# Attention softmax on one core: every second group's block maxima joined on GpSimd, head by head, instead of on VectorE

## What is computed

```python
q = (x @ Wq + bq).reshape(1, B * N, H, hd)             # 2048 queries, H = 16 heads, hd = 16
kv = (cond @ Wkv + bkv).reshape(1, -1, 2, H, hd)       # 2048 keys and values
...
attn = jnp.einsum('bhqk,bhkd->bhqd', q, k)             # each query against all 2048 keys
attn = jax.nn.softmax(attn.astype(jnp.float32), axis=-1)
attn = _fq_unsigned(attn, axis=-1)                     # rounded to 0..255 of the row's largest weight
out = jnp.einsum('bhqk,bhkd->bhqd', attn, v)
```

## Time and profile before

| | |
|---|---|
| median of 3 runs | 1166.4 us (1164.74 to 1167.02) |
| the profiled execution: its own time | 1166.14 us |
| its span, first to last instruction | 1164.4 us |
| busy over the span | PE 90%, DVE 82%, ACT 77%, POOL 60% |
| busy from 300 to 400 us | PE 86.77, DVE 98.11, ACT 98.44, POOL 80.50 us of 100 |
| granted TensorE clock from 300 to 400 us | 1.00 of full |
| first and last exponential of the attention | 85.6 and 722.3 us |

### The profile page before, as it was taken

How to read it: one execution, slowest core, us unless ns; L and a number is a source line. 1 busy time by engine, 2 the same in 40 slices (tenths; PEclk the granted TensorE clock), 3 DMA queues, 4 the chain that set the end, 5 groups by cost and what they waited for, 6 DMA issues and landing times.

```text
span 1164.4 us, 24047 instructions
## 1 busy us (share of the span) xinstructions
PE 1048.7 (90%) x8281; PEld 606.3 (52%) x8396; DVE 950.6 (82%) x1748; ACT 891.8 (77%) x1546; POOL 701.3 (60%) x625
## 2 busy tenths in 40 slices
PE   8988888888888888888888889899998999999997
PEld 4743444444444444444444447656654465557775
DVE  6999999999999999999999996863336788953335
ACT  4779999999999999999999996734543576834441
POOL 3016888888777878888788776447651000753332
PEclk9999999999999999999999999899999999999999
DMA  6697998888888889888876764856938001523336
GB/s 193 120 163 149 173 172 162 169 169 171 167 172 175 165 166 170 178 162 170 155 118 111 115 109 78 243 170 181 321 115 331 0 1 46 178 84 109 97 97 233
DMA packets 388799, 176.36 MB, mean 151 GB/s; under 512 B 330413, under 2 KB 373650, under 8 KB 388680
## 3 DMA queue, kind: packets, MB, share of 16 engines
q1 hardware_dynamic: 381976, 157.85, 62.1%
q0 software_dynamic: 6480, 16.77, 4.3%
q10 hardware_dynamic: 224, 0.20, 0.1%
HBM read 52.70 MB, written 43.59 MB: 83 GB/s over the span
## 4 chain that ended last, share of the span: by engine, by line
PE 49%; DVE 28%; ACT 13%; issue 5%; DMA 2%; POOL 2%; SPq 1%; ACTq 0%; POOLq 0%; DVEq 0%
DVE top L426 22%; ACT weight L485 10%; PE bank L220 8%; PE bank L234 8%; PE bank L1187 4%; PE bank L2616 4%; PE bank L1580 3%; PE bank L252 3%; PE bank L2632 3%; PE bank L1166 2%; PE bank L1174 2%; PE bank L1853 1%; PE bank L1598 1%; PE bank L682 1%; POOL dispatched_rows L1823 1%
## 5 line engine op out<-in xcount | busy, mean ns | idle before, releaser
L485 ACT ACTIVATE weight<-bank,bias,sq_all 128x1024 uint8<-128x1024 f32 x512 | 609.9, 1201 | 24.0 <-PE bank L234 18.7
L426 DVE TENSOR_REDUCE top<-bank 128x1 f32<-128x512 f32 (+1 forms) x683 | 610.2, 951 | 11.5 <-PE bank L220 1.1
L537 POOL CAST weight<-turned 128x2048 bf16<-128x2048 uint8 x256 | 478.8, 1892 | 41.0 <-PE bank L252 22.2
L234 PE MATMUL bank<-kT,query 128*128 128x512 bf16 x917 | 284.1, 382 | 26.4 <-ACT weight L485 12.2
L252 PEld LDWEIGHTS bank<-v_sb,weight 128*128 128x128 bf16 x4096 | 172.0, 96 | 102.7 <-POOL weight L537 0.5
L220 PE MATMUL bank<-kT,qspace 64*128 64x512 bf16 x687 | 135.0, 387 | 55.8 <-DVE top L426 55.8
L252 PE MATMUL bank<-v_sb,weight 128*128 128x16 bf16 x4096 | 172.6, 170 | 0.8 <-POOL weight L537 0.4
L220 PE MATMUL bank<-kT,query 128*128 128x512 bf16 x329 | 124.8, 379 | 2.1 <-DVE top L426 1.4
L234 PEld LDWEIGHTS bank<-kT,query 128*128 128x128 bf16 x1024 | 59.9, 97 | 103.9 <-ACT weight L485 61.9
L1823 POOL DMA_INDIRECT dispatched_rows<-qspace,put x32 | 37.1, 1160 | 116.0 <-DVE qspace L2373 106.9
L485 ACT ACTIVATION_READ_ACCUMULATOR weight<-bank,bias,sq_all 128x1 f32 x512 | 101.7, 199 | 0.0
(11 more groups left out here) (352 smaller groups left out, 1471.7 us busy)
## 6 DMA issues: line engine op xcount, KB each, us to landing
dispatched_rows<-zeros SPq DMA_DIRECT2D x32, 524.0 KB, 3.1
answered_rows<-zeros SPq DMA_DIRECT2D x16, 512.0 KB, 3.2
late<-answered_rows SPq DMA_DIRECT2D x16, 512.0 KB, 6.3
erow<-dispatched_rows SPq DMA_DIRECT2D x39, 131.0 KB, 2.1
wgu<-in_L_ffn_w_gate SPq DMA_DIRECT2D x26, 176.0 KB, 3.8
wgu<-in_L_ffn_w_up SPq DMA_DIRECT2D x26, 176.0 KB, 3.7
query<-qspace SPq DMA_DIRECT2D x32, 128.0 KB, 3.1
turned<-weight SPq DMA_TRANSPOSE x256, 3.1
```

The costliest lines, as they stand in the source:

```text
L234: mm = pe.matmul(unit[u % 2][:, v * 512:(v + 1) * 512], query2[:, t % 2, h, :], kT[:, h // 2, first + v * 512:first + (v + 1) * 512], star ...
L426: ve.tensor_reduce(top[:, first:first + count], bank[:, first % 3:first % 3 + count, :], AX.X, ALU.max).then_inc(s_max, 1)
L485: ac.activation(weight8[:, n % BYTES, u * 1024:(u + 1) * 1024], unit[u], ACT.Exp, bias=bias[:, n:n + 1], scale=sq_all[:, n:n + 1], accum_o ...
L537: po.tensor_copy(weight[:, n % 3, :, :, :].rearrange("p c q two -> p (c q two)"), turned8[:, n % 3, :, :].rearrange("p c q -> p (c q)").bi ...
```

## The change

The groups with an even number are joined as before. Of a group with an odd number (32 of 65), VectorE's line 430 is gone, and so is GpSimd's multiplication of line 520. In their place GpSimd waits for VectorE's last reduction of that group, and then handles each head by itself, on one column per operation: the maximum of three block columns (one as the tensor, two as scalars per partition), and, after a wait for the last of these, the maximum with the fourth column times the negative scale (again two scalars per partition). The addition of ln 255 stays one operation for the group.

```diff
-            group_end = {last_reduction(NBLOCK * (n0 + k) - 1): (n0, k) for n0, k in group_of}
+            group_end = {last_reduction(NBLOCK * (n0 + k) - 1): (n0, k) for n0, k in group_of[::2]}
...
                 n0, k = group_of[i]
                 sh = shift[:, n0:n0 + k]
-                po.wait_ge(s_shift, i + 1)
-                po.tensor_tensor(sh, sh, nsq_all[:, n0:n0 + k], ALU.mult).then_inc(s_scaled, 1)
+                if i % 2 == 0:
+                    po.wait_ge(s_shift, i // 2 + 1)
+                    po.tensor_tensor(sh, sh, nsq_all[:, n0:n0 + k], ALU.mult).then_inc(s_scaled, 1)
+                else:
+                    po.wait_ge(s_max, last_reduction(NBLOCK * (n0 + k) - 1) + 1)
+                    columns = {n: [top[:, 2 * NBLOCK * (n // 2) + 2 * b + n % 2:][:, 0:1] for b in range(NBLOCK)] for n in range(n0, n0 + k)}
+                    for n in range(n0, n0 + k):
+                        m = po.tensor_scalar(shift[:, n:n + 1], columns[n][0], columns[n][1], columns[n][2], ALU.max, ALU.max)
+                    m.then_inc(s_joined, 1)
+                    po.wait_ge(s_joined, i // 2 + 1)
+                    for n in range(n0, n0 + k):
+                        m = po.tensor_scalar(shift[:, n:n + 1], shift[:, n:n + 1], columns[n][3], nsq_all[:, n:n + 1], ALU.max, ALU.mult)
+                    m.then_inc(s_scaled, 1)
                 po.wait_ge(s_scaled, i + 1)
                 po.tensor_scalar(bias[:, n0:n0 + k], sh, LN255, None, ALU.add).then_inc(s_bias, 1)
```

More of the change, by code:

```diff
@@ L173, in program @@
             s_blk, s_max = sem("score_blocks_for_maximum"), sem("maxima_taken")
-            s_shift, s_scaled, s_bias = sem("group_maxima_joined"), sem("shifts_scaled"), sem("biases_ready")
+            s_shift, s_joined, s_scaled, s_bias = sem("even_group_maxima_joined"), sem("odd_group_maxima_joined"), sem("shifts_scaled"), sem("biases_ready")
             s_unit, s_exp = sem("score_units_ready"), sem("exponentials_finished")
```

## The result

The changed kernel takes 1195.78 us (median of 5 runs, 1194.86 to 1196.78) against 1166.4 us: 29.4 us more, a ratio of 1.0255 with a 95% interval of 1.0244 to 1.0266. The forecast was 1204 us, slower, range 1177 to 1236. The forecast had added up 37.9 us. Its profiled execution has a span of 1193.4 us, 29.0 over that of before.

A forecast was written before the change was run, and what follows sets the result against it. Attention was taken as bound by the ping-pong between VectorE, ScalarE and TensorE's fixed order. 31 late casts losing 1.22 us each, 37.9 us, on 1166.4 gave 1204.3, stated as 1204 us, range 1177 to 1236.

The forecast's parts named there:

- The joinings at nothing: VectorE's 32 removed joinings of line 430, at most 4.8 us, would gain nothing, hidden in a 0.15 us gap per round.
- s: Start-to-start time of GpSimd's new one-column operations with two scalars per partition: 0.34 us, bounded by 0.20 and 0.46.
- D: Delay of GpSimd's cast behind an odd group's biases: 8s - 0.19 us, put at 2.53, between 1.41 and 3.49.
- The distances: From cast end to TensorE's first weight load of that head, 0.10 to 2.16 us: how much later the cast may come.
- the six kinds: Heads 99, 107, 115, 123, 131, 139 stand for all 31 late casts, as TensorE's order repeats every 48 heads.
- The 0.15 us that a stall absorbs: VectorE's unused time per round, taken off each delay; the rest of a stall is lost and never caught up.
- Casts behind the late one at nothing: Following GpSimd casts start late but recover in 71.6 us of waiting and 41.0 us of idle time; no loss counted.
- 16.2 us of work in 19.6: GpSimd's load per eight heads: 8 casts at 1.89 us and two pairs of small operations at 0.56 us.
- A short chain: GpSimd's small operations overlap, s near 0.1 and D 0.61, losing 4 us: 1170 us; chance 0.07.
- VectorE as the bound: VectorE gives back its removed joinings, 4.8 us less: 1161.6 us; chance 0.03.
- a slow path: Scalars per partition slow on GpSimd, s from 0.75, loss 140 us: 1306 us; chance 0.08 with anything over 1234.
- Rival 4: TensorE's own waits for VectorE absorb 0.3 us per stall, not 0.15: loss 33 us, 1199 us; within the 0.82 case.

The follow-up runs named there:

- the two quarters: Changed kernel's one-piece joining on GpSimd for every fourth group alone: groups 3, 7, 11 and so on took 1171.66 us, groups 1, 5, 9 and so on 1186.04 us.
- the eight operations behind the biases: Kernel before plus eight unread one-column GpSimd operations after the biases, ahead of the cast of heads with n % 8 = 3: 1223.0 us.
- the fourth turned buffer: Changed kernel with four buffers of turned bytes, so the transposing DMA of head n waits for the cast of head n - 4, not n - 3: 1191.09 us.
- the run without joinings: Changed kernel with odd groups joined on no engine, GpSimd multiplying the first block's maxima alone: 1168.2 us.
- the version in three pieces: Changed kernel with an odd group's eight small operations spread ahead of three casts (one head, one head, last two heads): 1188.49 us.
- without the additions: The version in three pieces without GpSimd's 16 additions of the projection's bias to x: 1178.13 us.
- twelve operations: Changed kernel with the joining's first step done twice, the first time into an unread buffer, so twelve small operations ahead of the late cast: 1249.22 us.

## Why the prediction was right, and where its size was off

**Mechanism.** TensorE's value steps wait for the late casts, and VectorE and ScalarE stand behind TensorE. The stall of head 139 shows the chain, and the two quarters (5.5 and 19.9 us) show that it goes by the distance at the head. What the forecast had no term for is TensorE's clock behind a stall, some 4.5 us.

**The joinings at nothing.** Right: with 32 of them gone and nothing in their place the attention ends at 722.2 us, as before at 722.3.

**s, the price of an operation.** Forecast 0.34 us. Four take 1.40 us, the last 0.366, so they start (1.40 - 0.37) / 3 = 0.345 apart. If the second ALU step costs nothing, which no run separates, each of the two scalars costs about 0.07 on 0.22. The estimate from the Trainium skill's read commands (GPSIMD Engine Reference, Performance pitfalls for Q7 kernels), 0.255, is too low as I had counted them.

**How much later: the term that was mis-sized.** I took the time from VectorE's last reduction to the cast as 0.73 us before, and D as 2.53. The reduction that I took for the group's last, at 405.77, is the one *behind* it: line 430 stands one reduction further on, because it joins the group of reduction r - 1 after reduction r. The earlier trace rows show it: of the merged pair from 403.95, the first, until 405.18, was the last of the group. The changed kernel waits for the reduction itself, and so starts 0.6 us earlier, or 1.14 us where a pair follows. At head 139, VectorE's last reduction ends at 434.94 and the cast starts at 436.27 before, 1.33 us, against 454.72 - 451.33 = 3.39 us after: D = 2.06. That the head start is what was missing is shown by the eight operations behind the biases: without it heads 43, 91 and their like are late by 2.67 us and not 2.01, and the kernel loses 56.7 us and not 29.4, some 5 to 8 us of the difference by the clock; late biases play no part there.

**The distances.** From the end of the group's last reduction to the first weight load, the heads of the six kinds came later by these means over their five or six occurrences: kind 99 (3, 51, 99 ...) 0.06, 107 1.41, 115 0.41, 123 1.69, 131 0.16, 139 2.01 us. Forecast were 0.31, 1.23, 0.71, 2.28, 0.43, 2.37. The order is right, the sum 5.74 and not 7.33. Over the 31 heads it is 28.7 us. That this is so near to the measured 29.4 is chance: it is how late the loads come, not what is lost, and a part that stalls absorb and the clock that they cost nearly cancel (see the next two paragraphs).

**The 0.15 us that a stall absorbs.** Right in kind, and on the small side. Where the clock stays at 2.4 GHz, the load seven heads on is later by less than the stalled load was: 1.8 for 2.01 us at head 91, 1.53 for 1.75 at head 107, 1.56 for 2.12 at head 123. So 0.2 to 0.55 us are absorbed. At head 139 the attention is later by 3.1 us for a load that is 2.01 late, which hides it; the stretch at 1.2 GHz is the difference. It has no term in the forecast.

**Casts behind the late one at nothing.** Wrong, and hidden by the first error. With D as measured and nothing else, the kinds would lose about 0, 0.8, 0.3, 1.1, 0.0 and 2.0 us, 4.2 in the place of 5.74, some 22 us. The other 7 us of lateness come from GpSimd reaching the joining late. At head 107 VectorE's last reduction lies 4.27 us ahead of the cast, and not 3.39, and GpSimd has no idle time between the casts and the joining:

```profile
364.03 5.57 POOL L548 CAST weight<-turned 128x2048 bf16<-128x2048 uint8 x3 [1.51 <-DMA turned<-weight]
369.59 1.40 POOL L526 TENSOR_SCALAR shift<-top 128x1 f32<-128x1 f32 x4
```

I had 16.2 us of work in 19.6 and forgot the addition to x (0.73 us) in two of eight casts of the first quarter; with it and the joining it is over 20. The wait of 1.51 us above is for the transposing DMA. This DMA behind the late cast, which I had called hidden, is worth 4.7 us (the fourth turned buffer).

**The rivals.** A short chain (1170), VectorE as the bound (1161.6) and a slow path (1306) are out by s = 0.345 and the run without joinings. Rival 4, more absorption than 0.15 us, is in part right: 0.2 to 0.55 us a stall, as read above. It doesn't explain the smaller loss by itself, since the clock took nearly as much again, and D was 2.06 and not 2.53.

**Still open** is why TensorE's clock falls behind some stalls and not behind others of the same length (139 and 91); what a stretch at 1.2 GHz costs is read from like heads, and no run changes the clock alone. Open is also how the loss of the version in three pieces splits after the first quarter (about 9.6 us without the additions). It has stalls at heads 11, 27, 43 and their like, where the cast comes without idle time before it, but no run separates the load from the distance there. No version that I tried beats the kernel before, and the run without joinings says that there was nothing to gain by moving the joinings.

## What to carry to other kernels

Before work goes to an engine that is 60% busy, look at who waits for what that engine does next, and read the distance for each place in the period of the pattern, not on average: here it was 0.1 us at one head and 2.2 us at another, and the same operations cost 5.5 or 19.9 us. Measure the distance from the event that the new code waits for, found in the order of the program, not from the neighbour of the instruction that goes. After the change, read the granted clock beside the waits: behind four of the stalls here TensorE ran for 3.4 us at 1.2 GHz, at some 1.1 us each, so a waiting time by itself doesn't give the price of a stall. And look whether the instruction that goes costs time at all: two adjacent rounds, one with it and one without, told that in two rows.

## What I had not expected of the hardware

A GpSimd operation on one column with two scalars per partition took 0.366 us, against 0.22 us for four columns with an immediate, and its neighbours start 0.345 us apart: small operations of this kind hardly overlap. Casts next to them stayed at 1.891 to 1.896 us, and VectorE's reductions at 0.951 to 0.952 us on average, with any of these kernels' work on GpSimd.

TensorE's granted clock fell to 0.50 for 3.4 us behind idle times of its matmuls of 1.45 to 1.64 us (heads 43, 139, 187 and 219 of the changed kernel), in an attention whose clock otherwise is at 1.00, and such a stretch cost 0.9 to 1.3 us. With longer or more stalls there was more of it: 34.1 us of the attention with the eight operations behind the biases, 68.3 us with twelve operations, none in the kernel before.
